# In-chunk matmuls placed round the four column strips of TensorE, and issued for two slots at a time

## What is computed

```python
z, xBC, dt_raw = split(u @ in_proj_w.T)
x, B, C = split(silu(conv4(xBC) + conv_b))           # 1024, 128 and 128 channels
dt = softplus(dt_raw + dt_bias);  dA = dt * -exp(A_log)
# for every chunk z of 64 tokens and every head h:
Y_diag = einsum('zcn,zsn,zhcs,zshp->zchp', C, B, L, x * dt)   # L = exp of differences of cumsum(dA), causal
states = einsum('zcn,zch,zchp->zhpn', B, decay_to_chunk_end, x * dt)
Y_off  = einsum('zcn,zhpn,zch->zchp', C, state_before_chunk, exp(cumsum(dA)))
y  = (Y_diag + Y_off + x * D) * silu(z)
x1 = layernorm(u + (y * rsqrt(mean(y*y) + eps) * norm_weight) @ out_proj_w.T)
h  = silu(x1 @ w_gate.T) * (x1 @ w_up.T)             # weights unpacked from 4 bits
out = layernorm(x1 + rmsnorm(h @ w_down.T))
```

## Time and profile before

| | us |
|---|---|
| median of 3 runs (2022.22 to 2026.64) | 2024.91 |
| the profiled execution | 2034.44 |
| its span in the trace | 2032.5 |
| PE busy in the span | 1847.0 |
| DVE busy | 1419.1 |
| POOL busy | 983.9 |
| ACT busy | 921.0 |

### The profile page before, as it was taken

One profiled execution on the slowest core, in us unless ns is written; L12 is line 12 of the kernel. 1 busy time (PEld: TensorE's weight loads), 2 busy tenths in 40 slices (PEclk: granted clock), 3 DMA queues, 4 the chain that ended last, 5 costly groups with the idle time before them and its releaser, 6 DMA issues. The chain is left out here.

```text
span 2032.5 us, 37312 instructions
## 1 busy us (share of the span) xinstructions
PE 1847.0 (91%) x11168; PEld 986.0 (49%) x11168; DVE 1419.1 (70%) x2295; ACT 921.0 (45%) x1647; POOL 983.9 (48%) x1031
## 2 busy tenths in 40 slices
PE   3699999989998998998999899898999999999998
PEld 1255555646545555554654555655334334334333
DVE  6758668666857766875875676875776766765765
ACT  2453354253444334425334434423664654754753
POOL 0045345434525434542542543555764764764754
PEclk9899999999999999999989999889999999999999
DMA  6110140131122014113012201813010110110110
GB/s 200 46 45 25 40 104 26 34 75 39 43 48 80 24 45 101 25 39 86 28 42 55 68 24 50 212 34 71 7 57 32 34 59 26 36 62 26 36 42 31
DMA packets 212566, 109.54 MB, mean 54 GB/s; under 512 B 131642, under 2 KB 183542, under 8 KB 212390
## 3 DMA queue, kind: packets, MB, share of 16 engines
q1 hardware_dynamic: 212390, 107.37, 19.8%
HBM read 80.57 MB, written 26.76 MB: 53 GB/s over the span
## 5 line engine op out<-in xcount | busy, mean ns | idle before, releaser
L1015 ACT ACTIVATE decay<-ps_d 128x512 f32<-128x512 f32 x256 | 151.7, 593 | 383.1 <-PE ps_d L766 381.8
L777 PE MATMUL ps_yd<-mix,xpad 128*32 128x64 f32 x4096 | 281.6, 226 | 31.7 <-DVE y L1326 30.7
L777 PEld LDWEIGHTS ps_yd<-mix,xpad 128*32 128x32 f32 x4096 | 242.6, 113 | 122.6 <-issue 93.2
L1600 POOL TENSOR_TENSOR xend<-xpad,decay 128x256 f32<-128x256 f32 x256 | 180.6, 725 | 228.3 <-PE ps_yo L799 198.2
L708 PE MATMUL ps_in<-u_hi,w_hi 128*128 128x512 f16 (+1 forms) x608 | 238.5, 392 | 52.8 <-DVE u_lo L1188 32.3
L1290 DVE TENSOR_TENSOR mix<-decay,gb 128x512 f32<-128x512 f32 x256 | 222.4, 874 | 54.9 <-ACT gb L1002 31.9
L708 PE MATMUL ps_in<-u_lo,w_hi 128*128 128x512 f16 (+1 forms) x608 | 237.7, 391 | 0.0
L708 PE MATMUL ps_in<-u_hi,w_lo 128*128 128x512 f16 (+1 forms) x608 | 236.9, 390 | 0.0
L730 PE MATMUL ps_in<-w_out,zg 128*128 128x512 f32 x512 | 230.8, 604 | 6.7 <-DVE pre L1201 6.7
L1201 DVE SCALAR_TENSOR_TENSOR pre<-ps_in,cws,pre 128x511 f32<-128x511 f32 (+2 forms) x240 | 178.8, 745 | 14.2 <-ACT pre L954 8.4
L954 ACT ACTIVATE pre<-ps_in,cb,cws 128x512 f32<-128x512 f32 x80 | 62.2, 777 | 231.9 <-PE ps_in L708 231.9
(11 more groups left out here) (194 smaller groups left out, 3877.2 us busy)
## 6 DMA issues: line engine op xcount, KB each, us to landing
ebc<-e_dram SPq DMA_DIRECT2D x256, 64.0 KB, 2.6
u<-u_t SPq DMA_DIRECT2D x9, 1024.0 KB, 5.1
res<-u_tok SPq DMA_DIRECT2D x32, 256.0 KB, 2.7
x_dram<-res SPq DMA_DIRECT2D x32, 256.0 KB, 2.0
xa<-x_dram SPq DMA_DIRECT2D x8, 1024.0 KB, 6.1
xr<-x_dram SPq DMA_DIRECT2D x32, 256.0 KB, 2.7
out<-xr SPq DMA_DIRECT2D x32, 256.0 KB, 2.0
fw_words<-gu_words SPq DMA_DIRECT2D x32, 176.0 KB, 2.7
```

The lines of the kernel that those rows point to most:

```text
L777: last = mm(ps_yd[g * 32:(g + 1) * 32, k * CH:(k + 1) * CH], xpad[:, c % 2, k * NG + g, :], mix[:, g, k, :], start=True, stop=True, tile_p ...
L1015: ac(decay[:, n % NG, :, :].rearrange("p a b -> p (a b)"), ps_d[n % 2][:, :], ACT.Exp).then_inc(e_done, 1)
L1600: g_.tensor_tensor(xend[:, g:NP:NG, :], xpad[:, c % 2, g:NP:NG, :], decay[:, g, :, CH - 1:CH].broadcast_to([P, CT, 2 * HD]), ALU.mult).the ...
```

## The change

The 32 pairs are numbered anew. Before, group `g` had the pairs `g, g+4, g+8, ...`, and all its outputs lay in strip `g`. Now group `g` has the pairs `8g` to `8g+7`. They fill two whole column blocks of `ps_yd`, and one after the other go to strips 0, 1, 2, 3, 0, 1, 2, 3. What the first matmul of `exponents` reads is laid out to fit: the table is stored in DRAM with eight DMAs of 8 partitions each where two of 32 partitions stood (per half of the tokens), and the constant block `rhs_d` is loaded by ten DMAs where two did it. And `within` is no longer called in every slot: in slots with even `g` it is left out, and in slots with odd `g` it is called for the slot before and for this one, in one burst, behind that slot's projection.

```diff
-        ld_dram = nc.dram_tensor("ld_dram", [nb, 3, NP, 2, L], BF16, kind="Internal")
+        ld_dram = nc.dram_tensor("ld_dram", [nb, 3, CT, NG, 2, L], BF16, kind="Internal")
...
                     for h2 in range(2):
-                        sp.dma_start(ld_dram[b, :, :, h2, t].rearrange("r q t -> q r t"),
-                                     ld_parts[row + h2 * NP:row + (h2 + 1) * NP, :, :]).then_inc(parts_out, 16)
+                        for j in range(NG):
+                            heads = slice(row + h2 * NP + j * CT, row + h2 * NP + (j + 1) * CT)
+                            sp.dma_start(ld_dram[b, :, :, j, h2, t].rearrange("r e t -> e r t"), ld_parts[heads, :, :])\
+                              .then_inc(parts_out, 16)
...
-            later += [(rhs_d[6:94, i, :, :], c_rhs) for i in range(2)]
+            later += [(rhs_d[6:30, i, j * CT:(j + 1) * CT, :], c_rhs[0:24].rearrange("r (e j) t -> r j e t", j=NG)[:, j])
+                      for i in range(2) for j in range(NG)]
+            later += [(rhs_d[30:94, i, :, :], c_rhs[24:24 + CH]) for i in range(2)]
...
                 mm(ps_d[n % 2][:, :].rearrange("p (k t) -> p k t", k=CT), lhs_d[0:94, c % 2, g, :],
-                   rhs_d[0:94, c % 2, g:NP:NG, :], start=True, stop=True).then_inc(d_full, 1)
+                   rhs_d[0:94, c % 2, g * CT:(g + 1) * CT, :], start=True, stop=True).then_inc(d_full, 1)
...
-                for k in range(CT):
-                    last = mm(ps_yd[g * 32:(g + 1) * 32, k * CH:(k + 1) * CH], xpad[:, c % 2, k * NG + g, :],
-                              mix[:, g, k, :], start=True, stop=True, tile_position=(0, g * 32))
+                for e in range(CT):
+                    tile, strip = 2 * g + e // NG, e % NG
+                    last = mm(ps_yd[strip * 32:(strip + 1) * 32, tile * CH:(tile + 1) * CH],
+                              xpad[:, c % 2, g * CT + e, :], mix[:, g, e, :], start=True, stop=True,
+                              tile_position=(0, strip * 32))
...
                     use_in(st, n)
-                    within(b, n)
+                    if g % 2 == 1:
+                        within(b, n - 1)
+                        within(b, n)
                     if g == 1 and c > 0:
                         from_before(b, c)
...
-                g_.tensor_tensor(xend[:, g:NP:NG, :], xpad[:, c % 2, g:NP:NG, :],
+                pairs = slice(g * CT, (g + 1) * CT)
+                g_.tensor_tensor(xend[:, pairs, :], xpad[:, c % 2, pairs, :],
```

More of the change, by code:

```diff
@@ L404, in build @@
         GU_ORDER = [("g", 0), ("g", 1), ("u", 0), ("u", 1), ("g", 2), ("u", 2), ("g", 3), ("u", 3)]
-        N_SMALL, N_CONST = 16 * 5, 16 * 9
+        N_SMALL, N_CONST = 16 * 5, 16 * 17
+        PARTS_OUT = 16 * 18
         E_OUT, EBC_IN = 16 * 8, 16 * 8
@@ L497, in load_rows @@
                 sp.dma_start(lhs_d[6:30, c % 2, :, :].rearrange("r g (h s) -> r (g h) s", h=2),
-                             ld_dram[b].rearrange("r (q g) h t -> (r q) (g h) t", g=NG)[:, :, t])\
+                             ld_dram[b].rearrange("r e j h t -> (r e) (j h) t")[:, :, t])\
                   .then_inc(rq_in[c % 2], 16)
@@ L545, in load_head @@
             def load_head(b):
-                sp.wait_ge(parts_out, (b + 1) * 96)
+                sp.wait_ge(parts_out, (b + 1) * PARTS_OUT)
                 settled(sp)
@@ L557, in room_free @@
                 sp.wait_ge(u_max, nb + 1)
-                sp.wait_ge(parts_out, nb * 96)
+                sp.wait_ge(parts_out, nb * PARTS_OUT)
             def load_weights(step):
@@ L1237, in dt_second @@
                     ch.step(v.tensor_tensor_scan(dte[:, :], mask[:, :], dtb[:, :], 0.0, ALU.mult, ALU.add))
-                    need(dve, parts_out, b * 96)
+                    need(dve, parts_out, b * PARTS_OUT)
                     ch.step(v.tensor_copy(cs_parts[:, 0, :], dte[:, :]))
@@ L1414, in body @@
                 if st.kind == "last":
-                    dve.wait_ge(parts_out, nb * 96)
+                    dve.wait_ge(parts_out, nb * PARTS_OUT)
                     turn(0, range(KT))
```

## The result

The changed kernel takes 2007.9 us (median of 4 runs, 2006.9 to 2011.34) against 2023.76 (4 runs) of the kernel before: ratio 0.9907, 95% interval 0.9878 to 0.9936. (The ratios on record are not the quotients of the two medians; here that quotient is 0.992, and elsewhere in this document too it differs by up to 0.003.) By the medians it is faster by 16 us where 60 were forecast, and outside the range of 1935 to 2000. Its profiled execution took 2006.9 us, with a span of 2005.1; TensorE's mean granted clock is 0.919 where it was 0.969.

What follows compares the result with a forecast made beforehand. PE (busy 91%) was taken to bound the kernel except where it waits for DVE or SP's table; 7.0 us for each of bodies 1 to 6, 9.5 for body 0, 8 for body 7, rounded 60, gave 1965, range 1935 to 2000.

Steps and rivals of the forecast that it cites:

- The spacing: In-chunk matmuls on PE: 0.028 us from start to start with rotating strips, not 0.056; a burst takes 1.02 us.
- That rival: In-chunk bursts: four strips side by side, 0.014 us spacing, burst 0.57 us, 18 us more gain, 1947; chance 15%.
- the row of the seam: Two slots back to back, two strips in flight: 1.71 us, one matmul start per 0.028 to 0.03 us.
- Slots 12 and 13, and 20 and 21: PE from the end of the `y_all` wait to `from_before`: gains of 0.8 and 2.5 us a body.
- the full stretch before: Stretch ahead of slot 12 with DVE busy 13.56 of 14.77 us: `y_all` no earlier, stretch about as long as before.
- the clock's rival: Longer PE waits leave TensorE at 1.2 GHz; 7 us more low-clock work a body eats the gain, twice that 2081; 5%.
- the sign of being wrong: Whole kernel: the prediction is wrong if TensorE's mean granted clock falls below 0.95.
- The wait for `lhs_d` at slot 5: PE waiting for chunk 2's exponents' table: grows from 3.9 to some 7 us in bodies 2 to 6; gain 0.
- SP's stores: Twelve more store DMAs per sequence, 6.4 us on SP, covered by its wait until 565.06: cost 0.
- the wait of `from_before` for the state: At slots 13 and 21 a new wait for the state appears, about 1 us at each.
- The rival that the rotation gives nothing: In-chunk matmuls: spacing stays 0.056 us, only the burst is left, 19 us gain in all, 2006; chance 10%.

Runs made afterwards that it cites:

- 12 stores: Kernel before, exponents' table stored by eight DMAs of 8 partitions in place of two of 32, old layout kept: 2012.1 us, ratio 0.9893.
- 24 increments: Kernel before with 24 more semaphore increments on SP ahead of the table's stores, no DMA more: 2014.2 us, ratio 0.9938.
- the long gap back: Changed kernel with 24 more semaphore increments on SP, behind the stores of the next sequence's tables: 2018.1 us, ratio 0.9953 to the kernel before.
- the rotation alone: Changed kernel with `within` issued in each slot again, so no burst: 2025.3 us, ratio 0.998 to the kernel before.
- the last version: Changed kernel with 12, 12, 18 idle matmuls, and second-slot exponents and transposes (chunks 1 to 7) moved behind the burst: 1949.1 us, ratio 0.9601.

## Why the prediction was wrong

The positions of `from_before` cut body 3 into four parts, which can be set against the terms of the sum:

| from, to | before | after | difference | forecast | before, short gap (12 stores; 24 increments) |
|---|---|---|---|---|---|
| first `new_state` to slot 13 | 41.2 | 36.0 | -5.2 | -1.8 | 35.5; 35.5 |
| slot 13 to slot 21 | 38.5 | 37.4 | -1.1 | -3.5 | 38.5; 39.2 |
| slot 21 to slot 29 | 33.2 | 35.9 | +2.7 | -1.0 | 33.2; 37.0 |
| slot 29 to the next body | 54.5 | 56.4 | +1.9 | -0.7 | 54.8; 54.8 |
| sum | 167.4 | 165.7 | -1.7 | -7.0 | 161.9; 166.5 |

The 5.2 us of the first part are SP's shorter turn, which no term had: the kernel before takes 35.5 us there too once its gap is short. With the long gap PE waits 3.91 us at slot 5 and then runs at 0.51 from 622.59 to 627.65; with the short one (12 stores) neither is left:

```profile
616.37 0.39 PE L769 MATMUL ps_d<-rhs_d,lhs_d 94*128 94x512 bf16 x1 [0.30 <-DMA lhs_d<-ld_dram]
```

Why the last column has 33.2 in one run and 37.0 in the other is again the clock: in the second, behind the same wait of 2.86 us at slot 20, it stays low for longer, and `o1` lasts 8.61 us and not 7.03.

*The spacing* was wrong, in the kernel's favour. Rows of 32 last 0.65 us with the last one's 0.22: (0.65 - 0.22) / 31 = 0.014 us from start to start, four strips side by side, at full clock. That is a mean: the trace has four starts 0.007 apart and the next four some 0.037 later, so 0.056 for a round of four. A burst takes 0.59 us to the start of what follows, not 1.02. I took 0.028 as the bound nearest to the row of the seam; at that seam only two strips could ever be in flight, so it couldn't speak on four. That rival had 15%, and its mechanism held; its 1947 didn't.

*Slots 12 and 13, and 20 and 21* were rightly sized where I looked. From the end of the wait to `from_before` are now 1.70 and 1.71 us (649.14 to 650.84, 686.54 to 688.25) for 2.81 and 4.25: gains of 1.1 and 2.5, forecast 0.8 and 2.5. That `y_all` would come no earlier held too: 17.3 us after the start of the full stretch before (637.69 to 654.95), 17.7 after (631.45 to 649.14). But the full stretch itself was not as long as before, as I had it: cut at `new_state` it fell from 14.77 to 11.79 us. PE ran ahead, and what DVE had left to do moved behind the next `new_state`, where DVE is now busy 18.59 us and not 15.95.

*The step that failed* is the price of the stretches with the gain 0, and what I let follow on them at slots 12 and 20: I wrote "Now the state, ended by DVE at 693.63, sets the start of `from_before`" and took the work behind it as unchanged. From `from_before` to the end of `o0` are 12.9 us (650.84 to 663.76) where they were 9.4 (657.76 to 667.21), and as much more at slot 20. I had in the row the wait of 2.86 us that was followed by a low clock, and forecast that the wait for `y_all` would shrink. It couldn't: with DVE fixed, each us that PE saves ahead of it is a us more of waiting. At slot 12 a wait of 1.06 us became two, of 1.24 and 2.42; at slot 20 2.86 became 1.92 and 2.48; and at slot 28 no wait became 0.41 and 3.68. "Gain 0, DVE is full" was the wrong price for these stretches: the wait is free, the clock behind it costs about 4 us. At three places that is some 12 us a body, of which the kernel before paid one or two in body 3, and more in bodies 1 and 5 (`o1` 8.3 us).

*The balance of body 3*: in-chunk work took 32.0 us (30 slots of 1.01 and 1.71 for the pair of slots that stood together), and takes 16 x 0.59 = 9.4; PE's busy time falls only from 156.2 to 145.7, so some 12 us of lower clock have come back. They lie at the three places and, less, at the start of the body: at its turn into the next one PE runs at 0.50 from 774.55 to 780.55, behind a wait of 1.84 us for ACT's `xpad`, and the kernel before has only the stretch behind slot 5. PE's idle time rises from 11.2 to 20.0. So 22.6 saved, 12 lost to the clock, 9 to waits.

*The clock's rival* ("Slower, through the clock", 5%) had the mechanism, with its price too low and one of its places wrong. It put 7 more us of work a body at the low level, and looked at slot 5. The mean clock fell to 0.919, below the 0.95 that I had named as the sign of being wrong. It didn't end slower, since the strips saved more than I thought and the gap on SP gave some 10 us. Those 10 of the measured 16 us are luck: no term of mine had them. Against the kernel before with a short gap (2012.1 and 2014.2) nothing is left that can be told.

*The wait for `lhs_d` at slot 5* did not grow to 7 us; it fell to 1.99 in body 3. PE loses 2.02 us at 609.20 to ACT's `xpad`, and runs at a lower clock from there; and SP's turn is 2.4 us shorter. With the long gap back the wait is 3.76 us, about what it was: the bursts of slots 0 to 4 did not bring PE there earlier. Their gain was 0, but not for the reason that I gave, that the same DMA covers it.

*SP's stores* cost nothing, as forecast, but with nothing to spare: they last from 548.31 to 558.96, and the packed weights' transfers follow at once, where SP stood until 565.06. I said that SP would still wait there; it doesn't.

```profile
548.31 0.73 SPq L449 DMA_DIRECT2D cs_dram<-cs_parts  x1
549.15 3.70 SPq L454 DMA_DIRECT2D ld_dram<-ld_parts  x8
...
553.80 5.16 SPq L454 DMA_DIRECT2D ld_dram<-ld_parts  x8
559.31 0.38 SPq L528 DMA_DIRECT2D fw_words<-gu_words  x1
```

*DVE's work* as a whole weighs the same (it is busy 1419.8 us, was 1419.1), and the wait of `from_before` for the state appeared as forecast (0.6 to 1.1 us). The rival that the rotation gives nothing fell in its mechanism, though the rotation alone gave no time. Body 7, given 8 us, took 112.6 us from its first `new_state` to the first matmul of the feed-forward layer, where it took 120.2.

Shown by runs: that the strips overlap; the gap on SP and what it is worth; and that idle work in the waits makes the changed kernel faster, by 30 us, and by 59 together with the new order. Argued from rows alone: that the clock costs some 12 us in each body, the split of body 3 into 12 and 9, and that the kernel before gains less from idle work. Open: what in SP's stream makes its turn long, how the last version's gain divides, and which waits bring the clock down.

## What to carry to other kernels

A saving on an engine that then waits for a fixed partner is not just worth nothing: on TensorE the longer wait can lower the clock for the work behind it. So for each wait that a change lengthens, cost the instructions behind it at both levels of the clock, and place other work into the wait, or idle matmuls if there is none; how many are enough has to be measured. And before a gain of under 1% is put down to an edit, look at the turns of the loops on the engines that only issue DMAs: an unrelated instruction may have moved them.

## What the runs showed of the hardware

- Matmuls of 128 rows by 32 columns with 64 columns streaming (fp32, two passes each) start every 0.014 us on average if they go round the four column strips (four starts 0.007 apart, the next four 0.037 later), and every 0.056 us in one strip. The Trainium skill (TensorE: Matmul & The Clock Gate, Wait — 56ns, not 53.3ns?) has start-to-start never below about 25 ns; here the measurement decides.
- Waits of 1.24 and 2.42 us, 1.1 us of short work apart, were followed by a clock of 0.50. With 1.24, 0.35 and 1.05 us, and 2.33 us of idle matmuls behind the first, it fell behind slot 12 in five bodies of seven. With 1.24, 0.65 and 0.24 us, and 2.76 us of them, it fell there in none. So equal waits can end either way.
- SP's turn of a hardware loop takes 0.75 or 3.1 to 3.4 us in the same program, by a few instructions more or fewer elsewhere in its stream; 24 semaphore increments changed it in either direction, and twelve DMAs more made it short. The "q14 instruction" queue has 87 to 89 packets with the long turn and 63 with the short one.
